# A graph network's edge tables: the two halves' own terms stored as neighbouring rows, loaded and blanked in pieces of 2 KB

## The reference, cut to what matters

```
layer 3 (in the code: edges_3), for each edge:
    h      = relu(concat(x[src], x[dst]) @ W1 + b1)
    inter  = h @ W2 + b2
    gated  = inter * sigmoid(inter @ Wg + bg)
    pooled = segment_sum(gated, src) / max(count(src), 1)
layer 4 (edges_4), for each edge:
    g      = leaky_relu((x @ Wl + bl)[src] + (x @ Wr + br)[dst] + edge_attr_16 @ We)
    logits = sum over each of 4 heads of g * att
    alpha  = softmax of logits over the edges of one dst
    out    = segment_sum((x @ Wl + bl)[src] * alpha, dst) + bias, batch norm, gelu
```

## Time and profile before

| | |
|---|---|
| median of three runs | 6517.41 us |
| the profiled execution's own time | 6520.88 us |
| its span, first to last instruction | 6519.2 us |
| TensorE, weight loads | 3457.2 us (53%), 1973.1 us (30%) |
| VectorE, ScalarE, GpSimd | 3709.5 us (57%), 1754.1 us (27%), 3548.2 us (54%) |
| DMA packets | 1376052, 1051533 of them under 512 B |
| mean granted TensorE clock | 0.664 of full speed |

### The profile page before, as it was taken

How to read it: one execution, slowest core, us unless ns; L and a number is a source line. 1 busy time by engine, 2 the same in 40 slices (tenths; PEclk the granted TensorE clock), 3 DMA queues, 4 the chain that set the end, 5 groups by cost and what they waited for, 6 DMA issues and landing times. The chain is left out here.

```text
span 6519.2 us, 58257 instructions
## 1 busy us (share of the span) xinstructions
PE 3457.2 (53%) x12150; PEld 1973.1 (30%) x12150; DVE 3709.5 (57%) x4301; ACT 1754.1 (27%) x3305; POOL 3548.2 (54%) x3662
## 2 busy tenths in 40 slices
PE   3466656573434343333433433666776666666662
PEld 2344434241222222222222212333333333333331
DVE  9988955552333333333333333777777777777776
ACT  1233323361111111111111111333333333333332
POOL 5430033326666666666666656666666666666653
PEclk7566657785666666666666655677667767676675
DMA  8756457713434343333333412333333333333331
GB/s 196 205 192 200 149 148 195 123 29 89 101 97 105 96 102 101 101 97 102 102 98 97 103 48 62 84 85 85 86 83 87 85 85 85 84 87 85 85 82 33
DMA packets 1376052, 678.01 MB, mean 104 GB/s; under 512 B 1051533, under 2 KB 1254927, under 8 KB 1374994
## 3 DMA queue, kind: packets, MB, share of 16 engines
q1 hardware_dynamic: 1099684, 341.45, 22.5%
q0 software_dynamic: 116880, 124.33, 10.1%
q10 hardware_dynamic: 159390, 211.24, 9.3%
HBM read 344.06 MB, written 332.55 MB: 104 GB/s over the span
## 5 line engine op out<-in xcount | busy, mean ns | idle before, releaser
L1650 POOL DMA_INDIRECT got<-tabg,ix x1568 | 1483.4, 946 | 895.9 <-DMA t<-rows 454.4
L1456 POOL DMA_INDIRECT got<-tabg,ix x1568 | 1483.6, 946 | 829.8 <-issue 457.1
L1554 DVE TENSOR_TENSOR_SCAN own<-mk,own,p_first 128x512 f32<-128x512 bf16 x195 | 247.0, 1267 | 1128.9 <-remote 1011.8
L177 PE MATMUL p_out<-ident,run 128*128 128x128 f32 (+1 forms) x3136 | 672.6, 363 | 395.1 <-ACT rows L1514 155.6
L1476 PE MATMUL p_inter<-hid,W 128*128 128x512 f32 x392 | 306.7, 875 | 890.1 <-issue 715.9
L177 PEld LDWEIGHTS p_out<-ident,run 128*128 128x128 f32 (+1 forms) x3136 | 550.3, 216 | 718.0 <-issue 578.7
L1785 DVE TENSOR_TENSOR_SCAN top<-p_reset,top,logit 128x512 f32<-128x512 f32 x195 | 249.6, 1280 | 578.6 <-issue 252.3
L163 PE MATMUL p_small<-ident,ea 128*32 128x128 f32 (+1 forms) x784 | 175.4, 369 | 736.4 <-ACT rows L1748 702.5
L1523 ACT ACTIVATE hid<-pre,B 128x512 f32<-128x512 f32 x196 | 141.6, 722 | 1181.8 <-DVE pre L1570 529.2
L1478 PE MATMUL p_gate<-hid,WF 128*128 128x512 f32 x392 | 286.1, 821 | 263.2 <-issue 161.9
L493 DVE TENSOR_TENSOR_SCAN run<-p_mk,run,feat 128x512 f32<-128x512 f32 x302 | 370.5, 1269 | 61.3 <-remote 30.5
(11 more groups left out here) (347 smaller groups left out, 6736.0 us busy)
## 6 DMA issues: line engine op xcount, KB each, us to landing
t<-rows ACTq DMA_DIRECT2D x195, 512.0 KB
first<-start SPq DMA_DIRECT2D x780, 128.0 KB
t<-rows ACTq DMA_DIRECT2D x195, 288.0 KB
got<-tabg,ix POOLq DMA_INDIRECT x3136
start<-zeros SPq DMA_DIRECT2D x100, 500.0 KB
ea<-in_ea_dram SPq DMA_DIRECT2D x390, 128.0 KB
mk<-marks SPq DMA_DIRECT2D x780, 64.0 KB
start<-zeros SPq DMA_DIRECT2D x195, 256.0 KB
```

Of the source, the lines that this page charges most:

```text
L177: mm = nc.tensor.transpose(bank[0:g.p, cc, :], by_place(t, g)[:, :, cc], ident[:, :])
L1456: nc.gpsimd.indirect_dma_start(got[s][0:g.p, cc, h, :], None, tabg, bass.IndirectOffsetOnAxis(ap=ix[0:g.p, g.n, h, cc:cc + 1], axis=0)).th ...
L1650: nc.gpsimd.indirect_dma_start(got[s][0:g.p, cc, h, :], None, tabg, bass.IndirectOffsetOnAxis(ap=ix[0:g.p, g.n, h, cc:cc + 1], axis=0)).th ...
```

## The change

A table's row of edge r of half h is now 2r + h, so that the halves' rows alternate in the table as they do in the tile. A partition's eight rows, 2 KB, are one piece on both sides. Three things follow: `finish` works out the new row of a first edge; the two loads of `first` become one, and the blanking write of layer 3 takes 2 KB pieces (`zeros` is now flat); the waits' counts go with them (32 to 16, 80 to 64, and 23 to 24 for the added VectorE operation). The blanking of `start2` is as it was.

```diff
+def interleaved(table, row, width):
+    return table[ds(row, width), :].rearrange("(p k) f -> p (k f)", k=2 * C)
...
-                pool.wait_ge(ends.v, 23)
+                pool.wait_ge(ends.v, 24)
...   Ends.finish
-        nc.vector.tensor_scalar(self.f1[:, :], self.before[:, :], -float(NONE), None, ALU.add).then_inc(self.v, 1)
+        nc.vector.tensor_scalar(self.f1[:, :], self.before[:, :], 2.0, -float(NONE + 2 * H - 1), ALU.mult, ALU.add).then_inc(self.v, 1)
...
-        dve.wait_ge(self.v, 19)
-        nc.vector.tensor_tensor(self.f2[:, :], self.f1[:, :], self.has[:, :], ALU.mult).then_inc(self.v, 1)
+        nc.vector.scalar_tensor_tensor(out=self.f2[:, :], in0=self.s1[:, :], scalar=float(2 * H - 1), in1=self.f1[:, :], op0=ALU.mult, op1=ALU.add).then_inc(self.v, 1)
+        dve.wait_ge(self.v, 20)
+        nc.vector.tensor_tensor(self.f1[:, :], self.f2[:, :], self.has[:, :], ALU.mult).then_inc(self.v, 1)
...   edges_3, load
-                    s, m, row = g.slot(AHEAD), g.slot(MARKS), snapped(sp, g.row)
+                    s, m, row, pairs = g.slot(AHEAD), g.slot(MARKS), snapped(sp, g.row), snapped(sp, g.row * 2)
...
-                    for h in range(2):
-                        sp.dma_start(first[s][0:g.p, :, h, :], by_edge(start, h, row, g.w)).then_inc(first_in[s], 16)
-                    sp.dma_start(both_halves(next_start, row, g.w), zeros[0:g.p, :, :]).then_inc(blanked, 16)
+                    sp.dma_start(first[s][0:g.p, :, :, :].rearrange("p c h f -> p (c h f)"), interleaved(start, pairs, 2 * g.w)).then_inc(first_in[s], 16)
+                    sp.dma_start(interleaved(next_start, pairs, 2 * g.w), zeros[0:g.p, :]).then_inc(blanked, 16)
...   edges_3, first_rows
-                    pe.wait_ge(first_in[s], 32 * g.turn(AHEAD) + 32)
+                    pe.wait_ge(first_in[s], 16 * g.turn(AHEAD) + 16)
...   edges_4, load
+                    sp.dma_start(first[s][0:g.p, :, :, :].rearrange("p c h f -> p (c h f)"), interleaved(start, pairs, 2 * g.w)).then_inc(first_in[s], 16)
                     for h in range(2):
-                        sp.dma_start(first[s][0:g.p, :, h, :], by_edge(start, h, row, g.w)).then_inc(first_in[s], 16)
...   edges_4, first_rows
-                    pe.wait_ge(first_in[s], 80 * g.turn(AHEAD) + 80)
+                    pe.wait_ge(first_in[s], 64 * g.turn(AHEAD) + 64)
```

More of the change, by code:

```diff
@@ L817, in finish @@
         nc.vector.tensor_tensor(info["span"][:, :], self.s1[:, :], self.s2[:, :], ALU.mult).then_inc(self.v, 1)
-        dve.wait_ge(self.v, 19)
-        nc.vector.tensor_tensor(self.f2[:, :], self.f1[:, :], self.has[:, :], ALU.mult).then_inc(self.v, 1)
+        nc.vector.scalar_tensor_tensor(out=self.f2[:, :], in0=self.s1[:, :], scalar=float(2 * H - 1), in1=self.f1[:, :], op0=ALU.mult, op1=ALU.add).then_inc(self.v, 1)
+        dve.wait_ge(self.v, 20)
+        nc.vector.tensor_tensor(self.f1[:, :], self.f2[:, :], self.has[:, :], ALU.mult).then_inc(self.v, 1)
         nc.vector.tensor_tensor(self.l2[:, :], self.l1[:, :], self.has[:, :], ALU.mult).then_inc(self.v, 1)
-        dve.wait_ge(self.v, 21)
-        nc.vector.tensor_scalar(info["first"][:, :], self.f2[:, :], float(NONE), None, ALU.add).then_inc(self.v, 1)
+        dve.wait_ge(self.v, 22)
+        nc.vector.tensor_scalar(info["first"][:, :], self.f1[:, :], float(NONE), None, ALU.add).then_inc(self.v, 1)
         nc.vector.tensor_scalar(info["last"][:, :], self.l2[:, :], float(NONE), None, ALU.add).then_inc(self.v, 1)
@@ L1398, in edges_3 @@
     with Stage(nc) as c:
-        zeros = sb(c, "zeros", [P, 2, C * D])
+        zeros = sb(c, "zeros", [P, 2 * C * D])
         blank, blanked = sem(c, "blank"), sem(c, "blanked")
@@ L1533, in _ @@
                 nc.vector.memset(WG[:, :], 0.0).then_inc(zeroed, 1)
-                nc.vector.memset(zeros[:, :, :], 0.0).then_inc(blank, 1)
+                nc.vector.memset(zeros[:, :], 0.0).then_inc(blank, 1)
                 dve.wait_ge(folds, 1)
@@ L1615, in load @@
                 def load(g):
-                    s, row = g.slot(AHEAD), snapped(sp, g.row)
+                    s, row, pairs = g.slot(AHEAD), snapped(sp, g.row), snapped(sp, g.row * 2)
                     wait_from(sp, resets, g.n - AHEAD + 1)
                     wait_from(sp, owned, g.n - AHEAD + 1)
+                    sp.dma_start(first[s][0:g.p, :, :, :].rearrange("p c h f -> p (c h f)"), interleaved(start, pairs, 2 * g.w)).then_inc(first_in[s], 16)
                     for h in range(2):
-                        sp.dma_start(first[s][0:g.p, :, h, :], by_edge(start, h, row, g.w)).then_inc(first_in[s], 16)
                         sp.dma_start(ea[s][0:g.p, :, h, :], by_edge(ea16, h, row, g.w)).then_inc(first_in[s], 16)
```

## The result

The changed kernel took 6461.44 us, median of its runs (6446.71 to 6466.63), against 6517.63 us of the kernel before beside it: a ratio of 0.991 with a 95% interval of 0.990 to 0.992. That is 56 us faster, where 112 had been forecast.

What follows compares the result with a forecast made beforehand. GpSimd's gather pace, 10.0 us a group, plus 764 us of standing was taken to bound the edge loops; 6520.9 - 113 + 0.4 = 6408, set against the runs' median 6405 us, range 6165 to 6540, chance 0.43.

Steps and rivals of the forecast that it cites:

- What bounds the kernel: Edge loops: GpSimd's pace, 10.0 us a group, plus 764 us of standing for late-released consumers, not for data.
- The price of a piece: SyncE's queue: 97.8 ns for 2 KB; `first` falls from 20.2 to 12.5 us a group, zeros stay 12.5.
- slower rival: Edge loops: 2 KB pieces cost 178 ns and hold engines before gathers; 107 us slower, 6625 us; chance 0.14.
- my doubling: SyncE's queue: a 2 KB piece taken at twice the 1 KB piece's 48.9 ns, so 97.8 ns.
- From engine time to standing: Edge loops: standing falls in proportion to hardware queues' engine time, 0.150 x 345 + 0.147 x 419 = 113 us.
- Far more: Edge loops: SyncE's instruction rate (6188 us) or the packet count (6163 us) sets the standing; chance 0.22.
- SyncE's instruction rate: Layer 3's loop: 12 instead of 14 SyncE instructions a group take 10.08 us; 329 us off, 6188 us.
- the prediction's sign that SyncE had been the bound: Profile after: SyncE's wait grows while GpSimd keeps its pace of 1.25 us a gather.
- The number of packets: Edge loops: standing falls with packets, 59% in layer 3 and 36% in layer 4; 354 us off, 6163 us.
- Nothing: Edge loops: the stand is GpSimd's own doing; 6517 us within 13; chance 0.21, with not as said.
- The small terms: `finish`: one more VectorE operation of 128x49, twice, up to 0.4 us; scatter of start rows 0.

Runs made afterwards that it cites:

- four issues: Changed kernel with its load of `first` cut into four transfers by 32 partitions, still 128 pieces of 2 KB: 6421.45 us, 0.9909 of the kernel before.
- experiment 5: The changed kernel as it is, beside the kernel before on another chip with stands: 6416.97 us, ratio 0.9906.
- Experiments 8: Changed kernel loading 64 B a partition of `first` instead of 2 KB in the hardware loops, on a chip with stands: 6414.87 us, 0.9898 of the kernel before.
- experiment 10: Changed kernel with `first` landing in padded tiles in 512 pieces of 512 B, zeros leaving in 256 of 1 KB: 6487.53 us, 1.0012 of the kernel before.
- first cut: Changed kernel loading 64 B a partition of `first` instead of 2 KB: 5562.16 us (0.9999) on a chip without stands, 6414.87 us (0.9898) on one with.
- 512 pieces on the last: Changed kernel with `first` landing in a padded tile in 512 pieces of 512 B, one issue, on a chip without stands: 5559.65 us, 0.9998 of the kernel before.
- half the gathers: From the fifth group on GpSimd gathers only the first half's rows: kernel before 4783.38 us (0.7381), changed kernel 4759.48 us (0.734).

## Why the prediction was right in direction, and half wrong in size

*What bounds the kernel.* Right. GpSimd's pace of 1.25 us a gather is the floor: two chips ran both loops at exactly 10.0 us a group. And what is above it is standing, not TensorE's wait for data: with four issues that wait reached 766 us of 1600 and the loop took 2250 us, where the changed kernel's took 2244 on another chip.

*The price of a piece.* 97.8 ns had been taken for 2 KB; it was 112. So `first` fell from 20.2 us of engine time to 14.3, not 12.5, and the zeros rose from 12.5 to 14.3. In layer 4 the queue's time fell by 5.1 us a group, not 7.7, which makes a 2 KB piece 118 ns there. The nearest row in kind (a plain transfer of 1 KB, doubled) was a better guide than that of GpSimd's queue at 178 ns, on which the slower rival rested; it was 13% low.

The Trainium skill (DMA: Bandwidth & Descriptors, "Why small descriptors are slow") counts beats of 32 bytes and some three cycles a piece. From that comes an estimate of 67 against 11 cycles for 2 KB and 256 B, a ratio of 6.1, and of 35 / 11 = 3.2 for 1 KB. For 2 KB the traces agree better with it than with my doubling: 112 / 19.8 = 5.7 and 118 / 19.8 = 6.0, where I had 4.9. For 1 KB they don't: at most 48.9 / 19.8 = 2.5.

*From engine time to standing.* This is the step that failed: the standing time was taken to fall in proportion to the hardware queues' engine time. With the measured engine times the same working gives 3.9 / 51.4 x 345 + 5.1 / 52.4 x 419 = 26 + 41 = 67 us, just what the two loops gave, 43.7 + 23.2 = 66.9, and it would have been easy to stop there. By layer it has them the wrong way round, and the changed kernel's shares in experiment 5, 19.5% and 18.3%, are 35.8 and 35.0 us a group and would make it 21 + 32 = 53 us. Experiments 8 and 10 show the agreement to be chance: 14 us of engine time a group less moved nothing, and 512 pieces more at the same engine time took all of the gain. So the direction came true, and half of the size, but not by the mechanism that the forecast named: that much was luck. The reason given for the proportion, that layer 4 has 46% more packets and only 2% more engine time and stands 22% longer, compared two loops that differ in much else, and so the price of engine time was never isolated.

*Far more.* Both of its mechanisms are out at their prices. SyncE's instruction rate: six more instructions a group than the kernel before (four issues) did not bring its loops' length back. In the changed kernel SyncE waited more, 205.6 us instead of 16.6. That is the first half of the prediction's sign that SyncE had been the bound; the other half, GpSimd at its own pace, didn't come: it still stands. The number of packets: 1040 fewer of 1751 took 0.23 us off a stand of 1.76 us, 13% and not 59%, and experiment 10 has nothing won for the first 512 pieces of the way. That the number matters at all isn't shown.

*Nothing* was false on the chips with stands (the changed kernel at 0.991 twice, neither interval reaching 1) and true on those without, as far as its close variants say (0.9998 to 1.0007; the changed kernel itself wasn't run there). *Slower* was false: a 2 KB piece stayed under the 128 ns from which it would have decided. Whether one ever holds up a gather no row shows.

*The small terms.* `finish` has its added operation (timeline of VectorE). From `span` to `last` it starts them 0.83 us apart; before it was 0.71, from 337.41 to 338.12 us, beside the earlier trace rows. Twice that difference is 0.24 us, in place of 0.4:

```profile
338.07 0.20 DVE L822 TENSOR_TENSOR span<-s,s 128x49 f32<-128x49 f32 x1
338.19 0.20 DVE L823 SCALAR_TENSOR_TENSOR f<-s,f 128x49 f32<-128x49 f32 x1
...
338.90 0.18 DVE L829 TENSOR_SCALAR last<-l 128x49 int32<-128x49 f32 x1
```

*What stays open.* Why what TensorE signals comes late, and why the changed kernel gains. The runs show where it happens (with three sets of runs of five, most beside full-rate gathers, less beside half of them) and one change that moves it a little (768 pieces a group from SyncE in padded tiles against 256), not the shared thing itself. The remaining stand, 1.53 us a group in layer 3 and 2.02 in layer 4, some 695 us in all, is twelve times what the change won.

## What to carry to other kernels

A quantity that the profile lets you price to three digits is not by that the one that the wait answers to: before a gain is taken in proportion to something, find a run or a row in which that thing alone differs. Here the one experiment that cut the bytes and left the pieces (first cut) refuted the proportion at once, on a chip with stands. In this loop, whose stands begin and end with late releases and not with late data, merging small pieces into few of 2 KB helped by 1%; four issues of the same pieces cost nothing against one, and the bytes of a load didn't count. To find out whose release is late, take an engine that waits for one other only, and set its start beside the other's record. And before a loop is tuned against such stands, run it on a second chip: the same kernel had none there, and took 5564 us instead of 6481.

## What the runs showed of the hardware that was not expected

The kernel before took 6517.63, 6481.47 and 6478.21 us in three sets of runs and 5563.67 and 5559.78 us in two. The last four sets are from four different chips; which chip the first pair ran on isn't on record. The engines' own work is the same on both kinds: a gather has a median of 944 or 947 ns on each, and the scan of `own` takes 1.28 us. The mean granted TensorE clock of the profiled executions, between its two levels of 1.2 and 2.4 GHz, is 0.66 to 0.67 of full speed on the one kind with all gathers and 0.72 on the other. It doesn't explain the stands: TensorE's turns of `first` in 2000 to 3600 us take 273 ns in the median on both kinds, and with four issues 421 without a longer loop. What differs shows on SyncE's queue. The register operation beside the load of `first` (ns min/median/max, 2000 us on) in the changed kernel of the first pair:

```profile
L1447 SPq FUSED_REGOPS  x138: 3/52/1398, 2003.5 to 3580.9; - x138
L1447 SPq MOVE first<-start x138: 3/690/1390, 2004.3 to 3581.7; - x138
L1447 SPq DMA_DIRECT2D first<-start x138: 2/371/1406, 2005.0 to 3582.4; - x138
```

and with 512 pieces on the last:

```profile
L1454 SPq DMA_DIRECT2D first<-start x125: 576/577/862, 2001.9 to 3241.5; - x125
L1454 SPq FUSED_REGOPS  x124: 52/52/52, 2001.7 to 3231.9; - x124
L1454 SPq MOVE first<-start x124: 29/29/29, 2001.8 to 3232.0; - x124
```

A move that takes 29 ns every time on the last chip takes 3 to 1390 ns in the first pair, half of them 690 or more. With half the gathers, in the kernel before, some still take as long, as some releases are still late:

```profile
L1442 SPq MOVE first<-start x262: 3/29/1530, 1703.8 to 2499.6; - x131
```

So something delays single instructions of SyncE in three of the five sets of runs, and in the same three TensorE's signals come late. No run says whether the two have one cause, or whether it is the chip or its state at the time.
